# Layer 2's sums taken by ScalarE's relu in eight pieces, layer 1 in one PSUM bank, and single product tiles split in three passes

## The reference: what is computed

```python
def _cin(x, weights, biases):                      # x: 512 x 32 x 64
    for i, (w, b) in enumerate(zip(weights, biases)):
        z = jnp.einsum('bhd,bfd->bhfd', hidden, x).reshape(B, hidden.shape[1] * F, D)
        y = jax.nn.relu(jnp.einsum('bcd,oc->bod', z, w) + b[None, :, None])
        if i != n_layers - 1:
            hidden, direct = (y[:, :size // 2, :], y[:, size // 2:, :])
        else:
            direct = y
        finals.append(direct)
    return jnp.concatenate(finals, axis=1).sum(-1)  # 64 + 128 sums over d
```

## Time and profile before

| | |
|---|---|
| runs | 1070.89, 1071.25, 1071.31 us |
| profiled execution | 1070.25 us, of it span 1068.5 us |
| PE matmul busy | 1023.0 us (96%) |
| DVE busy | 931.2 us (87%) |
| POOL busy | 921.0 us (86%) |
| ACT busy | 724.6 us (68%) |
| DMA | 183.87 MB |

### The profile page before, as it was taken

One profiled execution on the slowest core, in us unless ns is written; L12 is line 12 of the kernel. 1 busy time (PEld: TensorE's weight loads), 2 busy tenths in 40 slices (PEclk: granted clock), 3 DMA queues, 4 the chain that ended last, 5 costly groups with the idle time before them and its releaser, 6 DMA issues.

```text
span 1068.5 us, 10631 instructions
## 1 busy us (share of the span) xinstructions
PE 1023.0 (96%) x3447; PEld 649.2 (61%) x3447; DVE 931.2 (87%) x610; ACT 724.6 (68%) x794; POOL 921.0 (86%) x300
## 2 busy tenths in 40 slices
PE   2299999999999999999999999999999999999999
PEld 1146556566666666666666666666666666666663
DVE  3079999999998999999999999999989888988881
ACT  5056666677767767776777677677777777777762
POOL 6528777799999999999999999999988988898980
PEclk9999999999999999999999999999999999999999
DMA  6488788778778777887787778777776687677630
GB/s 171 91 208 191 179 196 188 174 189 187 188 179 190 185 176 182 189 194 175 187 191 175 173 189 192 177 191 182 186 167 167 165 190 165 165 170 182 165 73 0
DMA packets 140633, 183.87 MB, mean 172 GB/s; under 512 B 55633, under 2 KB 56273, under 8 KB 140450
## 3 DMA queue, kind: packets, MB, share of 16 engines
q1 hardware_dynamic: 135986, 178.93, 70.7%
q0 software_dynamic: 4096, 4.20, 2.2%
q10 hardware_dynamic: 496, 0.06, 0.0%
HBM read 174.66 MB, written 8.39 MB: 171 GB/s over the span
## 4 chain that ended last, share of the span: by engine, by line
PE 94%; POOL 2%; issue 1%; DVE 1%; ACTq 1%; DMA 1%; ACT 0%; DVEq 0%
PE py L641 43%; PE py L657 16%; PE py L647 16%; PE py L648 16%; POOL emb L341 2%; PE py L662 1%; DVE zf L552 1%; ACTq L449 1%; PE py L676 0%; PE py L713 0%; PE pzS L713 0%; ACTq L221 0%; PE py L683 0%; DMA emb<-in_tbl,idx 0%; DMA idx<-in_ids 0%
## 5 line engine op out<-in xcount | busy, mean ns | idle before, releaser
L351 POOL TENSOR_TENSOR zl<-zf,zh 128x2048 fp32r<-128x2048 f32 x168 | 771.8, 4607 | 87.4 <-ACT zh L413 85.3
L552 DVE TENSOR_TENSOR zf<-xs,hid 128x2048 f32<-128x2048 f32 x256 | 582.9, 2282 | 50.7 <-ACT hid L428 46.8
L641 PE MATMUL py<-zf,wf 128*128 128x512 f32 x1080 | 485.1, 592 | 1.2 <-DVE zf L552 1.2
L413 ACT ACTIVATE zh<-zf 128x2048 fp32r<-128x2048 f32 x185 | 353.5, 1911 | 99.3 <-DVE zf L552 96.0
L641 PEld LDWEIGHTS py<-zf,wf 128*128 128x128 f32 x1080 | 204.3, 189 | 208.5 <-issue 194.7
L647 PE MATMUL py<-zh,wh 128*128 128x512 f32 x740 | 290.0, 392 | 1.3 <-ACT zh L413 1.3
L648 PE MATMUL py<-zh,wl 128*128 128x512 f32 x740 | 289.7, 392 | 0.0
L657 PE MATMUL py<-zl,wh 128*128 128x512 f32 x740 | 228.0, 430 | 0.0
L657 PEld LDWEIGHTS py<-zl,wh 128*128 128x128 f32 x740 | 139.4, 188 | 69.3 <-issue 46.6
L341 POOL DMA_INDIRECT emb<-in_tbl,idx x128 | 149.0, 1164 | 30.3 <-issue 25.5
L647 PEld LDWEIGHTS py<-zh,wh 128*128 128x128 f32 x740 | 139.0, 188 | 34.6 <-ACT zh L413 2.6
(11 more groups left out here) (79 smaller groups left out, 336.1 us busy)
## 6 DMA issues: line engine op xcount, KB each, us to landing
xs<-x_dram SPq DMA_DIRECT2D x512, 256.0 KB, 5.3
xs<-x_dram SPq DMA_DIRECT2D x504, 64.0 KB, 2.1
x_dram<-emb SPq DMA_DIRECT2D x66, 64.0 KB, 5.5
x_dram<-emb SPq DMA_DIRECT2D x22, 96.0 KB, 5.5
emb<-in_tbl,idx POOLq DMA_INDIRECT x128, 4.5
x_dram<-emb SPq DMA_DIRECT2D x4, 384.0 KB
xs<-in_L_rec_w SPq DMA_DIRECT2D x2, 512.0 KB, 4.6
xs<-in_L_rec_w SPq DMA_DIRECT2D x1, 1024.0 KB, 7.5
```

The lines of the kernel that those rows point to most:

```text
L351: pool.tensor_tensor(zl[:, q], zf[:, s], zh[:, q].bitcast(F32), ALU.subtract).then_inc(lo["P"], 1)
L413: act.activation(zh[:, q], zf[:, s], ACT.Copy).then_inc(hi, 1)
L552: dve.tensor_tensor(zf[:, slot(u)], left, right, ALU.mult).then_inc(mult, 1)
L641: mm = pe.matmul(y, wf[:, w, h], zf[:, s, h], start=first and h == 0, stop=ends and h == T - 1)
```

## The change

- `finish_2` becomes eight ACT instructions a group, one for each sample (128 by 64), each with the relu, the bias and an accumulator output that gives the sum over d; `sum_2` on DVE goes.
- Layer 1 has one bank `py1`. `finish_dir1` writes to a tile `dir1` in SBUF, even groups in one half of the partitions and odd ones in the other, and `sum_1` reduces 128 partitions once every two groups; two small ACT copies every 16 groups (`place_sums_1`) put the sums in place.
- The freed bank `pzB` takes tile 0 of some units (`through_bank`: C in 11 to 42, D in 11 to 62, P in 44 to 63). DVE writes that tile's product there as an instruction of its own, ACT rounds it (`high_bank`), DVE makes its low part (`low_bank`). For P and D, that tile goes from two fp32 records to three single passes; C had them already, and its low part for this tile moves from GpSimd to DVE. C is no longer V from group 11 on.
- At the start four warm-up multiplications instead of two, and they no longer wait for `x32_in`, only for the gathers of batch 2; two more pieces of weights are prepared.

```diff
     if name == "C" and g < 11:
         return "P" if g % 2 or g == 0 else "V"
-    if name == "C" and g < 43:
-        return "V" if g % 3 == 0 else "P"
     return "P"
+def through_bank(unit):
+    name, g = unit
+    return name == "P" and g > 43 or name == "C" and 11 <= g < 43 or name == "D" and 11 <= g < LAST
...
+            def high_bank(u):
+                if not through_bank(u):
+                    return
+                act.wait_ge(bank_mult, NTH_BANKED[u])
+                if u[0] not in OWN:
+                    act.wait_ge(used_split, NTH_SPLIT[u] - ZS)
+                elif NTH_OWN[u] > 1:
+                    act.wait_ge(used_own[u[0]], NTH_OWN[u] - 1)
+                act.activation(bank_parts(u)[0], pzB[:], ACT.Copy).then_inc(bank_hi, 1)
...
             def finish_2(g):
                 need_used(act, closing(g))
-                act.activation(py2[:, g % 2], py2[:, g % 2], ACT.Relu, bias=bias1[:]).then_inc(dir2_ready, 1)
+                for b in range(NS):
+                    part = py2[:, g % 2, D * b:D * b + D]
+                    act.activation(part, part, ACT.Relu, bias=bias1[:], accum_out=zsum2[:, NS * g + b:NS * g + b + 1]).then_inc(sum2_done, 1)
...
+                first = 1 if through_bank(u) else 0
+                if first:
+                    if NTH_BANKED[u] > 1:
+                        dve.wait_ge(bank_lo, NTH_BANKED[u] - 1)
+                    dve.tensor_tensor(pzB[:], left[:, 0], view(right, at, [[1, N]]), ALU.mult).then_inc(bank_mult, 1)
+                dve.tensor_tensor(zf[:, slot(u), first:T], left[:, first:T], view(right, at, [[0, T - first], [1, N]]), ALU.mult).then_inc(mult, 1)
...
+            def low_bank(u):
+                if not through_bank(u):
+                    return
+                dve.wait_ge(bank_hi, NTH_BANKED[u])
+                high_part, low_part = bank_parts(u)
+                dve.tensor_tensor(low_part, pzB[:], high_part.bitcast(F32), ALU.subtract).then_inc(bank_lo, 1)
...
                 products(("A", g))
-                sum_1(g)
+                low_bank(("D", g - 1))
+                if g % 2:
+                    sum_1(g // 2)
...
                 if g + 1 < G:
+                    low_bank(("P", g + 1))
                     low_s(g + 1)
                 products(("B", g))
-                if g >= 1:
-                    sum_2(g - 1)
+                low_bank(("C", g))
                 low(("C", g))
                 products(("D", g))
-            sum_2(LAST)
...
-                if name == "P" and g >= 2:
-                    pe.wait_ge(swapped, 3 * (g - 1))
-                    pe.wait_ge(sum1_done, g - 1)
+                if name == "P" and g >= 1:
+                    pe.wait_ge(swapped, 3 * g)
+                    pe.wait_ge(dir1_ready, g)
                 if name == "A" and g >= 2:
-                    pe.wait_ge(sum2_done, g - 1)
+                    pe.wait_ge(sum2_done, NS * (g - 1))
...
             pe.wait_ge(turns_ready, 1 + T + 2)
+            pe.wait_ge(gathered[2], gathered_count(2))
+            warm_up(4, py1[:])
             pe.wait_ge(x32_in, 16 * (2 * NS + 5))
-            warm_up(2, py1[:, 0])
             pe.wait_ge(x32_last, 16 * 3)
...
```

More of the change, by code:

```diff
@@ L84 @@
 NTH_SPLIT = {u: i + 1 for i, u in enumerate(SPLIT)}
+BANKED = [u for u in UNITS if through_bank(u)]
+NTH_BANKED = {u: i + 1 for i, u in enumerate(BANKED)}
+OWN = "PD"
+NTH_OWN = {u: i + 1 for name in OWN for i, u in enumerate(v for v in BANKED if v[0] == name)}
 NTH_LOW = {u: i + 1 for m in "PV" for i, u in enumerate(LOW[m])}
@@ L412, in high @@
                     act.wait_ge(used_split, i - ZS)
-                act.activation(zh[:, q], zf[:, s], ACT.Copy).then_inc(hi, 1)
+                first = 1 if through_bank(u) else 0
+                act.activation(zh[:, q, first:T], zf[:, s, first:T], ACT.Copy).then_inc(hi, 1)
+            def high_bank(u):
[7 more added lines that the diff above has]
+                act.activation(bank_parts(u)[0], pzB[:], ACT.Copy).then_inc(bank_hi, 1)
             def high_s(k):
@@ L425, in finish_straight, with place_sums_1 @@
                 else:
-                    act.wait_ge(w_low, 3)
-                act.activation(hid[0:H, 0], py1[0:H, k % 2], ACT.Relu, bias=bias0[0:H]).then_inc(straight, 1)
-                act.activation(hid[H:P, 0], py1[0:H, k % 2], ACT.Relu, bias=bias0[0:H]).then_inc(straight, 1)
+                    act.wait_ge(w_low, 5)
+                act.activation(hid[0:H, 0], py1[0:H], ACT.Relu, bias=bias0[0:H]).then_inc(straight, 1)
+                act.activation(hid[H:P, 0], py1[0:H], ACT.Relu, bias=bias0[0:H]).then_inc(straight, 1)
             def finish_dir1(k):
-                act.activation(py1[H:P, k % 2], py1[H:P, k % 2], ACT.Relu, bias=bias0[H:P]).then_inc(dir1_ready, 1)
+                if k >= 2:
+                    act.wait_ge(sum1_done, k // 2)
+                half = slice(H * (k % 2), H * (k % 2) + H)
+                act.activation(dir1[half, :], py1[H:P], ACT.Relu, bias=bias0[H:P]).then_inc(dir1_ready, 1)
+            def place_sums_1(c):
+                act.wait_ge(sum1_done, GC // 2 * (c + 1))
+                for odd in range(2):
+                    act.activation(view(zd, H * zd[:].ap[0][0] + P * c + NS * odd, [[2 * NS, GC // 2], [1, NS]], H),
+                                   sums1[H * odd:H * odd + H, H * c:H * c + H].rearrange("p (j b) -> p j b", b=NS),
+                                   ACT.Copy).then_inc(sums1_placed, 1)
             def finish_swapped(k):
@@ L435, in finish_swapped @@
                     act.wait_ge(mult, NTH["D", k - 1])
-                act.activation(hid[0:F, 1], py1[F:H, k % 2], ACT.Relu, bias=bias0[F:H]).then_inc(swapped, 1)
-                act.activation(hid[F:H, 1], py1[0:F, k % 2], ACT.Relu, bias=bias0[0:F]).then_inc(swapped, 1)
+                act.activation(hid[0:F, 1], py1[F:H], ACT.Relu, bias=bias0[F:H]).then_inc(swapped, 1)
+                act.activation(hid[F:H, 1], py1[0:F], ACT.Relu, bias=bias0[0:F]).then_inc(swapped, 1)
                 act.wait_ge(swapped, 3 * k + 2)
@@ L540, in products @@
                     dve.wait_ge(x0_ready, g)
-                    left, right = xd[g % 2], view(px0, 0, [[0, T], [1, N]])
+                    left, right, at = xd[g % 2], px0, 0
                 else:
@@ L550, in products @@
                         dve.wait_ge(xe_in, 16 * T * (g + 1))
-                    left, right = (xe if HALF[name] else xd[g % 2]), view(hid, N * SWAP[name], [[0, T], [1, N]])
-                dve.tensor_tensor(zf[:, slot(u)], left, right, ALU.mult).then_inc(mult, 1)
+                    left, right, at = xe if HALF[name] else xd[g % 2], hid, N * SWAP[name]
+                first = 1 if through_bank(u) else 0
+                if first:
[3 more added lines that the diff above has]
+                dve.tensor_tensor(zf[:, slot(u), first:T], left[:, first:T], view(right, at, [[0, T - first], [1, N]]), ALU.mult).then_inc(mult, 1)
             def products_s(k):
@@ L572, in low, with sum_1 @@
                 dve.tensor_tensor(zl[:, q], zf[:, s], zh[:, q].bitcast(F32), ALU.subtract).then_inc(lo["V"], 1)
-            def sum_1(k):
-                dve.wait_ge(dir1_ready, k + 1)
-                dve.tensor_reduce(zd[H:P, NS * k:NS * k + NS], py1[H:P, k % 2].rearrange("p (b d) -> p b d", d=D),
+            def sum_1(j):
+                dve.wait_ge(dir1_ready, 2 * j + 2)
+                dve.tensor_reduce(sums1[:, NS * j:NS * j + NS], dir1[:].rearrange("p (b d) -> p b d", d=D),
                                   AX_X, ALU.add).then_inc(sum1_done, 1)
[L579 to L582, removed]
             products(("P", 0))
@@ L620, in bank @@
             def bank(u):
-                return (py1 if u[0] == "P" else py2)[:, u[1] % 2]
+                return py1[:] if u[0] == "P" else py2[:, u[1] % 2]
             def main(u):
@@ L635, in main @@
                         pe.wait_ge(mult, NTH[u])
-                    for h in range(T):
+                    first_tile = 1 if through_bank(u) else 0
+                    for h in range(first_tile, T):
                         if u == ("P", 0) and h < T - 1:
@@ L640, in main @@
                             pe.wait_ge(mult, 1)
-                        mm = pe.matmul(y, wf[:, w, h], zf[:, s, h], start=first and h == 0, stop=ends and h == T - 1)
+                        mm = pe.matmul(y, wf[:, w, h], zf[:, s, h], start=first and h == first_tile, stop=ends and h == T - 1)
                     mm.then_inc(used_whole, 1)
```

73 lines of the change are left out of this document (59 added, 14 removed).

## The result

The changed kernel takes 1080.16 us (median of 6 runs, 1079.08 to 1081.69), the kernel before 1071.07 us beside it. The ratio is 1.0087, 95% interval [1.0071, 1.0103]. Slower was forecast, but at 1126 us. That the pieces lengthen the loop was right; what they cost was not, and in the middle groups, where half of the loss was forecast, there is none.

A forecast was written before the change was run, and what follows sets the result against it. PE was taken as the bound at 15.36 us a group, passed by the lengthened loop; +5.1, +26.9 and +25.6 for the stages with smaller terms made +54.8 on 1070.25, so a median of 1126 us, likeliest range 1090 to 1183.

The forecast's parts named there:

- The bound and the loop: PE bounds at 15.36 us a group; the loop product A, P, C, B, high B, finish_straight takes 14.43, 0.93 less.
- What PE saves: Split tiles take 0.17 us less each: PE needs 15.19 a group in groups 11 to 42, 15.02 in late groups.
- Y: Time of a group's eight ACT pieces, standing in the loop: 0.375 us each, 3.0 us taken, ends 1.2 and 4.6.
- the same formulas: Loop per group when ACT is late: 12.85 + Y to group 11, 13.20 + Y to 43, 13.64 + Y to 63.
- rival 2: ACT pieces: the sum is free but the bias is paid, Y = 2.24, 1081 us; chance 0.15 with everything towards rival 1.
- The sign of being wrong that I gave: The forecast is wrong if the pieces at L495 on ACT follow each other at under 0.25 us.
- DVE's terms: In the loop: sum_1 every second group -0.36 us, low_bank of D +0.72, split product +0.07, late low_bank of P +0.72.
- The cushion: At the end PE's lag of 3.0 us behind ACT's rounding of A is used up: -3.0 us.
- The start: Warm-up moved forward lets the spreads begin earlier, bounds -3.5 and 0: -1.0 us taken.
- Rival 1: ACT pieces are cheap, Y of 1.9 or less, deciding below 1.95: 1066 us, faster; chance 0.20.
- Rival 3: Reading the sum on ACT costs a lone record: Y = 4.6, 1227 us; chance 0.10 for Y above 3.9.
- Rival 4: PE waits and its clock falls, so the change doesn't save what it says; no chance of its own beyond rival 3's.

The follow-up runs named there:

- e3: The kernel before with only the eight pieces in finish_2 and sum_2 taken out, no bank, split tiles or new warm-up: 1084.71 us, ratio 1.0132.
- e2: The changed kernel with finish_2 one relu again and layer 2's sum a DVE reduce behind product B; bank and split tiles stay: 1066.16 us, ratio 0.9959.
- e5: The changed kernel with five of the eight pieces left between high C and high B, three moved behind the next high A: 1066.32 us, ratio 0.9965.
- e4: The changed kernel with the eight relus but without their accumulator output, layer 2's sums left out: 1065.48 us, ratio 0.9963.
- e6: e5 with P's tile through the bank only in every second late group, those without a sum_1: 1061.87 us, ratio 0.9922 to the kernel before.
- e8: The kernel before with only the start changed, four warm-up multiplications behind the gathers of batch 2: 1069.41 us, ratio 0.9997.

## Why the prediction was wrong, point by point

**The bound and the loop: right.** The changed trace shows the order product C, high C, pieces, high B, finish_straight, product A, with no wait of ACT behind high C, and e3 gives 15.54 where the loop's 14.43 with the pieces put on it makes 15.53. e2 and e5 confirm from two other sides that the pieces' place decides.

**What PE saves: right.** 0.17 a tile gives 15.19, and e2, e4, e5 and e6 all take 15.20 in the middle stage. The 15.02 of the late groups is not shown by any run: where P's tile is split in all of them (e2, e4, e5), the loop takes 15.27 without stray waits.

**The step that failed: Y, "I take 0.28 + 0.095 = 0.375, Y = 3.0".** Measured: 0.29 a piece, Y = 2.32. The read was sized well (0.09), but the piece costs 0.20 and not 0.28. I had taken the fixed part from two relus of 512 columns with a bias, 0.225, and the pieces show about 0.15 (0.20 less 0.055 for 64 columns). So a piece with its read costs about what I had taken for a piece with a free sum. With Y = 2.32 the same formulas give 15.17, 15.52 and 15.96 us: 0 (PE's 15.70 holds), +5.1 and +12.0, together +14.3 with the other terms, 1084.5 for this execution, where 1080.2 was measured. So Y makes 40.5 of the 44.8 us by which the forecast missed. The time is close to that of rival 2, 1081 with a Y of 2.24, but by luck: its reason, a free sum and the whole price of a bias, is not what e4 shows. It got a chance of 0.15 and should have had more, since ends of 1.2 and 4.6 were far apart and 0.1 us a piece is worth 50 us. The sign of being wrong that I gave, pieces at under 0.25 us, was set too low as well: 0.29 is Y = 2.32, already below the 2.4 at which my own range ended.

**DVE's terms: too dear by some tenths.** low_bank costs 0.60 in place of 0.72, product A before it 2.20 in place of 2.32, and the reduce 0.59 in place of 0.72 in every second turn: 0.30 a turn in all. By that the middle stage's turns are 15.22 on average where the formula has 15.52; late ones are 15.76 where it has 15.96. Stray waits add 0.14 in the middle stage: among them the two small copies of the sums. In the turn in which they stand (group 31) the pieces begin 0.67 us later and take 2.43:

```profile
537.84 0.65 ACT L466 ACTIVATE hid<-py,bias 64x512 f32<-64x512 f32 x1
...
549.35 0.53 ACT L479 ACTIVATE zd<-sums 64x64 f32<-64x64 f32 x2
...
554.14 0.66 ACT L466 ACTIVATE hid<-py,bias 64x512 f32<-64x512 f32 x1
```

This turn takes 16.30 where its neighbours with a sum_1 take 15.5: 0.8, not 0.3. The other stray waits, some 3 us in the middle stage, stand for the most part in front of product P, up to 0.5 us each; what ends them the trace doesn't tell.

**The cushion: not given back.** I had -3.0 at the end; behind group 63 the changed kernel gains 0.3. In its last group PE waits for A's high part and then for GpSimd's low part, which that cushion had covered:

```profile
1049.88 1.20 PE L731 MATMUL py<-zl,wh 128*128 128x512 f32 x4 [1.37 <-POOL zl L377]
```

**The start: right** in size (-1.3 against -1.0), though e8 can't tell it from nothing in the total.

**Rivals.** Rival 1 is what e4 shows when the read is taken away: at Y = 1.59 the time is the 1066 that it named. With the read Y is 2.32, so the change as it stands is not this case. Its threshold of 1.95 was not tested, and is too low: turns of 15.22 at Y = 2.32 put the point at which the loop passes PE's 15.19 near 2.3. Rival 3 is excluded: the read's record is 0.215 long but lies over its neighbours. Rival 4: the granted clock is 1.00 in the middle and the late stage of the changed kernel.

Left open: the late groups. In e2, e4, e5 and e6 several turns near group 48 take 15.8 to 16.8 us. In e6 DVE waits 3.6 us in all for loads of x between 760 and 850, in e5 4.4 in the late stage, in the changed kernel 0.4: the faster versions meet a limit there that the changed one hardly reaches. No run tested why.

## What to carry to other kernels

Ask of every instruction that is added which circle of waits it stands in, and what that circle takes without waits; find the turn in the trace in which the bounding engine was not waited for, and put the addition on it. The share of busy time (ACT 68% before) says nothing about it: eight small instructions cost this kernel some 14 us in one place of ACT's queue (e3 against the kernel before, the changed kernel against e2) and next to nothing with five there and three elsewhere (e5 against e2). When an instruction is moved out of a circle, write down the circle that it moves into as fully, with the matrix engine's passes in it. And where a price that no row shows is multiplied by 63, the forecast is only as good as that price: it should be given as the range that its ends make.

## What the runs showed that I had not expected

- A relu with an accumulator output is two instructions, ACTIVATE and ACTIVATION_READ_ACCUMULATOR. On 64 columns their records are 0.29 and 0.21 us long, but a pair takes only 0.29 from start to start, and without the read 0.20 (e4).
- Two relus of 512 columns with the same kind of bias stand 0.665 apart: 0.225 over their columns. In a row of small ones it is 0.15. The Trainium skill (ScalarE: Activation LUTs, What ACT_TABLE_LOAD costs) has 280 ns + 0.833 ns a column less 93 ns of overlap, an estimated 0.24 for 64 columns; the trace has 0.20 without the read.
- GpSimd's low part of 1536 columns takes 3.52 us against 4.61 for 2048, and in e6 it was busy for 468 of the middle stage's 486 us while PE's matmuls had no idle time there.
